# A one-core Perceiver block: more warming matmuls, head outputs in pairs, a 512-column weighted sum, and another order in the first group

## The reference, cut to what matters

```python
# layer 1
Q = layernorm(x) @ Wq + bq;  K = ctx @ Wk + bk;  V = ctx @ Wv + bv
attn = softmax(Q @ K.T) / 16
x = x + attn @ V
# layer 2, end of the delta rule: core has 8 heads of 128 x 128
core = core * rsqrt(mean(core * core, -1) + 1e-6) * gate_norm_w
core = core * silu(z)
h = resid + core.reshape(1, 128, 1024) @ W_out
```

## Time and profile before

| | |
|---|---|
| three runs | 228.18, 228.83, 229.16 us; median 228.83 us |
| profiled execution | 228.96 us, span 227.1 us |
| PE busy | 218.2 us (96% of the span), 1530 instructions |
| DVE busy | 146.8 us (65%), 349 instructions |
| ACT busy | 145.9 us (64%) |
| POOL busy | 133.4 us (59%) |
| DMA | 52.94 MB, mean 233 GB/s |

### The profile page before, as it was taken

One profiled execution on the slowest core, in us unless ns is written; L12 is line 12 of the kernel. 1 busy time (PEld: TensorE's weight loads), 2 busy tenths in 40 slices (PEclk: granted clock), 3 DMA queues, 4 the chain that ended last, 5 costly groups with the idle time before them and its releaser, 6 DMA issues.

```text
span 227.1 us, 4168 instructions
## 1 busy us (share of the span) xinstructions
PE 218.2 (96%) x1530; PEld 193.9 (85%) x1530; DVE 146.8 (65%) x349; ACT 145.9 (64%) x270; POOL 133.4 (59%) x87
## 2 busy tenths in 40 slices
PE   7999999999999999999999999959999999999994
PEld 6955888888888888989899999747899999999993
DVE  3035676666666666945996776775425579788783
ACT  3068777777778887636785676874327758677570
POOL 1045899888888888950599957390001525555550
PEclk9999999999999999999999999999999999999999
DMA  6999999999999901999700000000890677960000
GB/s 203 399 426 419 419 409 420 398 407 403 419 417 412 405 13 19 352 412 416 291 4 1 1 3 0 3 0 1 330 411 14 211 332 281 416 229 0 3 0 23
DMA packets 8532, 52.94 MB, mean 233 GB/s; under 512 B 953, under 2 KB 1217, under 8 KB 6466
## 3 DMA queue, kind: packets, MB, share of 16 engines
q1 hardware_dynamic: 8496, 52.68, 58.4%
q10 hardware_dynamic: 18, 0.01, 0.0%
HBM read 52.56 MB, written 0.13 MB: 232 GB/s over the span
## 4 chain that ended last, share of the span: by engine, by line
PE 78%; DVE 15%; ACT 3%; issue 2%; DMA 1%; POOL 0%; ACTq 0%; DVEq 0%
PE psum L507 24%; PE psum L599 13%; PE psum L873 8%; PE psum L502 7%; PE psum L575 6%; PE psum L735 3%; DVE work L1333 3%; PE psum L748 3%; PE psum L554 2%; PE psum L818 2%; DVE hh L1472 2%; DMA early_sb<-in_early 1%; PE psum L616 1%; PE psum L498 1%; DVE smalls L1222 1%
## 5 line engine op out<-in xcount | busy, mean ns | idle before, releaser
L405 POOL TENSOR_TENSOR ctx_lo<-ring,ctx_hi 128x1792 fp32r<-128x1792 f32 x13 | 52.6, 4044 | 13.8 <-ACT ctx_hi L943 13.8
L490 POOL TENSOR_TENSOR h_lo<-ring,h_hi 128x512 fp32r<-128x512 f32 x16 | 24.7, 1544 | 44.2 <-ACT h_hi L1162 38.1
L507 PE MATMUL psum<-xT,late_sb 128*128 128x128 f32 x224 | 26.4, 276 | 0.1
L507 PEld LDWEIGHTS psum<-xT,late_sb 128*128 128x128 f32 x224 | 25.6, 192 | 0.3 <-DVE xT L1529 0.3
L1222 DVE TENSOR_REDUCE smalls<-psum 128x1 f32<-128x896 f32 x14 | 15.3, 1092 | 15.3 <-PE psum L575 9.1
L507 PE MATMUL psum<-late_sb,work 128*128 128x448 f32 x60 | 24.7, 540 | 0.0
L950 ACT ACTIVATE probsT_hi<-psum 128x512 fp32r<-128x512 f32 (+1 forms) x26 | 12.7, 541 | 16.3 <-PE psum L502 16.3
L943 ACT ACTIVATE ctx_hi<-ring 128x1792 fp32r<-128x1792 f32 x13 | 22.1, 1701 | 0.0
L1246 DVE TENSOR_TENSOR probsT_lo<-psum,probsT_hi 128x512 fp32r<-128x512 f32 (+1 forms) x26 | 15.0, 619 | 6.6 <-ACT probsT_hi L950 6.6
L502 PE MATMUL psum<-early_sb,work 128*128 128x128 f32 x115 | 16.2, 274 | 0.3 <-DVE work L1457 0.2
L507 PEld LDWEIGHTS psum<-late_sb,work 128*128 128x128 f32 x60 | 10.5, 190 | 6.7 <-issue 6.7
(11 more groups left out here) (288 smaller groups left out, 522.9 us busy)
## 6 DMA issues: line engine op xcount, KB each, us to landing
late_sb<-in_ctx_T SPq DMA_DIRECT2D x14, 896.0 KB, 9.0
ring<-in_ctx SPq DMA_DIRECT2D x14, 896.0 KB, 7.8
late_sb<-in_late SPq DMA_DIRECT2D x10, 825.0 KB, 9.1
late_sb<-in_experts SPq DMA_DIRECT2D x8, 1024.0 KB, 6.0
late_slots<-in_experts SPq DMA_DIRECT2D x8, 1024.0 KB, 7.1
early_sb<-in_early SPq DMA_DIRECT2D x1, 512.0 KB, 3.8
early_sb<-in_early SPq DMA_DIRECT2D x1, 465.0 KB, 6.2
work<-in_levels SPq DMA_DIRECT2D x1, 416.0 KB, 7.3
```

What stands on the lines that cost most here:

```text
L405: nc.gpsimd.tensor_tensor(ctxNv[1][:, r % 2], ring[:, r], ctxNv[0][:, r % 2], ALU.subtract).then_inc(s["ctx_lo"], 1)
L490: nc.gpsimd.tensor_tensor(hT[1][:, e % 2, at, :], h32[:, at, :], hT[0][:, e % 2, at, :], ALU.subtract).then_inc(s["h_lo_done"], 1)
L507: last = nc.tensor.matmul(o, lhs(c), rhs(c), start=(c == 0), stop=(c == n - 1))
```

## The change: what it does

Four things are changed together.

1. `keep_warm(6)` before the rows becomes `keep_warm(7)` and `tick(2)`.
2. In the first group, ACT takes the exponential before `ctx_hi`. The group's `ctx_lo` is made by DVE and no longer by POOL, and POOL waits for it.
3. `ctx_hi` and `ctx_lo` lie side by side for each tile, so that one matmul of 512 columns takes hi*hi and hi*lo; lo*hi stays at 256 columns. The two halves of the bank are added by DVE in two steps, of which the second waits for the first. The last group is as before.
4. The head outputs go to four banks, in pairs. Gates and squares are done by pairs, the mean of squares of the first four heads stands ahead of the copy of the transposed heads, and PE projects the first heads before it transposes the second four.

```diff
-Y_BANKS = (0, 7, 1, 2, 3, 5, 4, 6)
+Y_BANKS = (1, 2, 5, 0, 6, 3, 7, 4)
+O_BANKS = (5, 0, 6, 7)
...
-            ctxN = parts(overlay, "ctx", 2 * GT * D)
+            ctxN = overlay.enter_context(nc.sbuf_tensor("ctx_parts", [P, 2 * GT * 2 * D], F32R))
...
+        def head_core(h):
+            return bank[O_BANKS[h // 2]][:, h % 2 * P:(h % 2 + 1) * P]
...
-            ctx_lo_parts(0, 0)
+            pool.wait_ge(s["ctx_lo"], 1)
...
-            keep_warm(6)
+            keep_warm(7)
+            tick(2)
...
+                def both(t):
+                    return nc.tensor.matmul(o[:, 0:2 * D], probsT[0][:, t, :], ctx_both[:, r % 2, t, :], start=(t == 0), stop=(t == GT - 1))
+
+                for q, tiles in ((1, range(4)), (2, range(4, GT))):
+                    pe.wait_ge(s["probsT_hi"], g * 2 + q)
+                    for t in tiles[:3 if q == 1 else 2]:
+                        both(t)
+                    pe.wait_ge(s["probsT_lo"], g * 2 + q)
+                    for t in tiles:
+                        nc.tensor.matmul(o[:, 0:D], probsT[1][:, t, :], ctxNv[0][:, r % 2, t, :], start=False, stop=False)
+                    last = both(tiles[-1])
                 last.then_inc(s["pv_done"], 1)
...
-                for k in range(4):
-                    last = nc.tensor.matmul(bank[5 + b][:, k * P:(k + 1) * P], Z[:, 4 * b + k, :], Bv[:, 4 * b + k, :], start=True, stop=True)
-                last.then_inc(s["o_mm"], 1)
...
+                for h in range(4 * b, 4 * b + 4):
+                    if h == 6:
+                        pe.wait_ge(s["zo_done"], 2)
+                        core_transposes(0)
+                    last = nc.tensor.matmul(head_core(h), Z[:, h, :], Bv[:, h, :], start=True, stop=True)
+                    if h % 2:
+                        last.then_inc(s["o_mm"], 1)
...
+            pe.wait_ge(s["coreT_dve"], 1)
+            for h in range(0, 2):
+                project_out(h)
+            pe.wait_ge(s["zo_done"], 4)
             core_transposes(1)
...
-            ctx_hi_parts(0, 0, 16, first=True)
             exps(0, 0, first=True)
+            ctx_hi_parts(0, 0, 16, first=True)
...
-            core_squares(0)
+            for pair in range(4):
+                core_squares(pair)
             act.wait_ge(s["core_T"], 2)
...
-            core_squares(1)
...
-                V.scalar_tensor_tensor(O[:, :], O[:, :], s_("al", b, b + 1), bank[6 + b][:, 0:D], ALU.mult, ALU.add).then_inc(s["acc_done"], 1)
+                link(V.scalar_tensor_tensor(O[:, :], O[:, :], s_("al", b, b + 1), bank[6 + b][:, 0:D], ALU.mult, ALU.add))
+                V.tensor_tensor(O[:, :], O[:, :], bank[6 + b][:, D:2 * D], ALU.add).then_inc(s["acc_done"], 1)
...
             sums(0, 0, first=True)
+            dve.wait_ge(s["ctx_hi"], 1)
+            V.tensor_tensor(ctxNv[1][:, 0], ring[:, 0], ctxNv[0][:, 0], ALU.subtract).then_inc(s["ctx_lo"], 1)
             probs_lo_parts(0)
...
-            gate_output(0)
-            gate_output(1)
+            for pair in range(3):
+                gate_output(pair)
+            mean_squares(0)
             dve.wait_ge(s["core_T"], 1)
...
-            mean_squares(0)
+            gate_output(3)
             dve.wait_ge(s["h0_done"], 1)
             for h in range(HV):
-                if h == 3:
+                if h == 2:
                     mean_squares(1)
```

More of the change, by code:

```diff
@@ L160, in perceiver @@
         probs = R2[:, 5888:5888 + GK]
-        ctxNv = [part[:, :].rearrange("p (b t d) -> p b t d", b=2, d=D) for part in ctxN]
+        ctx_both = ctxN[:, :].rearrange("p (b t e) -> p b t e", b=2, e=2 * D)
+        ctxNv = [ctx_both[:, :, :, part * D:(part + 1) * D] for part in range(2)]
         Tv = [part[:, :].rearrange("p (b c k) -> p b c k", b=2, c=DC) for part in T_parts]
@@ L592, in attend @@
                 pe.wait_ge(s["ctx_lo"], g + 1)
[L593 to L600, removed]
+                o = bank[6 + r % 2]
+                def both(t):
[8 more added lines that the diff above has]
+                    last = both(tiles[-1])
                 last.then_inc(s["pv_done"], 1)
@@ L758, in _, with core_transposes @@
                 last.then_inc(s["zt_mm"], 1)
+            def core_transposes(b):
+                transposes([(bank[3 + b][:, k * P:(k + 1) * P], core[:, 4 * b + k, :]) for k in range(4)], s["core_T"])
             for b in range(2):
@@ L951, in probs_hi_parts @@
                                          ACT.Copy).then_inc(s["probsT_hi"], 1)
+            exps(0, 0, first=True)
             ctx_hi_parts(0, 0, 16, first=True)
-            exps(0, 0, first=True)
             probs_hi_parts(0, first=True)
@@ L1103, in _, with core_squares @@
             nc.scalar.activation(Z[:, 4:8, :], bank[4][:, :].rearrange("p (h t) -> p h t", h=4), ACT.Copy, scale=-1.0).then_inc(s["zb_done"], 1)
[L1105 to L1108, removed]
+            def core_squares(pair):
+                act.wait_ge(s["zo_done"], pair + 1)
+                for h in (2 * pair, 2 * pair + 1):
+                    last = nc.scalar.activation(squares[:, h, :], head_core(h), ACT.Square, accum_out=s_("ms", h, h + 1))
                 last.then_inc(s["osq_done"], 1)
-            core_squares(0)
+            for pair in range(4):
+                core_squares(pair)
             act.wait_ge(s["core_T"], 2)
@@ L1452, in mean_squares, with gate_output @@
                                        ALU.mult, ALU.add).then_inc(s["ms_done"], 1)
[L1454 to L1457 removed]
+            def gate_output(pair):
+                dve.wait_ge(s["o_mm"], pair + 1)
+                dve.wait_ge(s["zs_done"], pair // 2 + 1)
+                at = slice(2 * pair, 2 * pair + 2)
+                V.tensor_tensor(core[:, at, :], bank[O_BANKS[pair]][:, 0:2 * P].rearrange("p (h t) -> p h t", h=2), zs[:, at, :],
                                 ALU.mult).then_inc(s["zo_done"], 1)
[L1460 to L1461 removed]
+            for pair in range(3):
+                gate_output(pair)
+            mean_squares(0)
             dve.wait_ge(s["core_T"], 1)
```

16 lines of the change are left out of this document (5 added, 11 removed).

## The result

The changed kernel took 226.63 us (median of five runs, 226.23 to 229.91) against 228.99 for the kernel before (228.18 to 229.16). The ratio is 0.9898, with a 95% interval from 0.9876 to 0.9920. That is faster by 2.4 us, where 223.5, 5.3 us less, was predicted. The direction held, and the time lies in the range, but the size was wrong by more than half.

The account below looks back on a forecast made before the run. PE was taken to bound the kernel, with 78% of the chain against DVE's 15%. From the profiled 228.96, less 3.6, 0.5 and 1.2, came 223.7, on the median's scale 223.5 us; range 222.8 to 228.1.

Parts of the forecast that it names:

- Part 3: The start: longer warming raises PE's clock early and the first group is reordered; 3.6 us gained.
- Part 1: The weighted sum with 512-column matmuls: 0.9 us gained over groups 0 to 10, 0.4 lost in group 11, so -0.5.
- a rise at 6.2: The start: if the clock's level rises only then, scores start at about 9.2 and the gain is 3.3 us.
- The early case that I took: The start: clock up while rows are transposed, scores from 8.44, gain 4.0 at best, 3.6 taken; chance 0.48.
- the new order: First group: late clock, no loss; early clock, exponential no longer held from 13.4 to 14.5, DVE's `ctx_lo` 2.3 us.
- The second addition: Steady groups on DVE: 0.44 us plus 0.03 wait, 0.47 more in a pause of 0.58, so hidden in groups 0 to 10.
- the rival in which it does not fit: Second addition on DVE takes 0.72 and overruns its pause: +2.6 us, 230.7 in all; chance 0.06.
- The saving per group: PE's weighted sum: seven pairs become seven 512-column matmuls, 0.08 us saved per group.
- PE's work behind the wait: End of layer 1: after `probsT_lo` of group 12 PE needs 1.74 us instead of 1.82, so 0.4 lost in all.
- Part 2: The head outputs in pairs, first mean ahead of the copy, earlier product with `W_out`: 1.2 us gained.
- The late rise: Rival at the start: the clock rises late all the same, 0.3 us lost there, 227.4 in all; chance 0.36.
- the heads gain little: Rival: late clock, and ACT or POOL's power holds the later sums, 0.9 of 1.2 goes, 228.3; chance 0.10.

Follow-up runs that it names:

- e1: The kernel before with only the longer warming at the start: 227.81 us against 228.51, ratio 0.9998.
- e4: The changed kernel with ACT's `ctx_hi` of the first group put ahead of the exponential again, DVE still making `ctx_lo`: 225.92 us, ratio 0.9929 to the kernel before.
- e6: The changed kernel with the whole old first group (`ctx_hi` first, `ctx_lo` on POOL): 226.11 us, ratio 0.9929 to the kernel before.
- e7: The kernel before with the new head outputs and the longer warming, old weighted sum and first group: 225.64 us, ratio 0.9881.
- e8: The changed kernel with layer 1's end reordered: `probsT_lo` ahead of the addition, last probabilities ahead of ACT's factor: 225.32 us, ratio 0.9879 to the kernel before.
- e11: The kernel before with the longer warming, the new head outputs and the reordered end of layer 1, old weighted sum and first group: 225.24 us, ratio 0.9871.
- e2: The kernel before with only the new head outputs in pairs, old short warming: 226.46 us, ratio 0.9938.
- e3: The kernel before with only the new 512-column weighted sum: 230.11 us, ratio 1.0104.
- e9: The kernel before with a write of zeros that nothing reads behind each DVE addition to `O`, 13 in all: 228.88 us, ratio 0.9990.
- e5: The changed kernel itself, run again on another set's chip: 226.67 us, ratio 0.9951 to the kernel before.

## Why the prediction was wrong in size

Of the 3.0 us that are missing, 1.8 are Part 3's and 1.1 Part 1's.

**Part 3 is the step that failed most: 3.6 predicted, 1.79 measured.** Two things were wrong in it. The first is the moment. I took a rise during the transposes and scores from 8.44; here it came after them, and the scores at 9.67, later than the 9.2 that I gave for a rise at 6.2. The 0.3 to 0.6 that the longer warming delays the transposes has to be paid in this case as well (0.49 here), and I had counted it only for the late rise. e1, with the same start and the old order, gains 2.61. The early case that I took does occur: in e4, e6, e7, e8 and e11 the two transposes start 0.27 or 0.28 apart and not 0.48. Even there the scores start at 8.82 to 9.20 and not at 8.44. The Trainium skill, in *TensorE: Matmul & The Clock Gate*, Part 1, says that the moment differs between runs of one kernel; the profiles agree, with scores from 8.82 to 12.00 behind the same warming.

The second is the new order, which I thought harmless or helpful. I had the first maximum ready at 13.4, where ACT's `ctx_hi` would still hold the exponential. For scores at 8.44 that was nearly right: in e2, with scores at 8.58, the maximum is ready at 13.67 and the exponential waits for `ctx_hi` until 14.01. With scores at 9.67 the maximum is ready only at 14.8, and `ctx_hi` fits ahead of it. What I had at nothing is the other side: with `ctx_hi` behind the exponential, POOL's next `ctx_lo` and `ctxT_lo` come 1.0 late, and `ctxT_lo` meets DVE's part of it. That cost 0.82 here, and 0.4 or more in every profile where DVE makes this `ctx_lo`. DVE's `ctx_lo` itself took 2.02, priced 2.3. Without the new order e2 reaches W1 at 25.09, 3.40 sooner than the kernel before, close to the 3.6: the rise was priced rightly for a lucky execution.

**Part 1, -0.5 predicted, +0.60 measured.** The second addition was right (0.42 against 0.44) and hidden in the steady groups as argued; the rival in which it does not fit is refuted. The saving per group was 0.06 on PE's weighted sum, not 0.08. The Trainium skill, in *TensorE: Matmul & The Clock Gate*, Part 1, has 2.5 ns a matmul; measured are 0.06 / 7, some 9 ns, nearer to the 12 taken from rows. Of the groups' 0.9 only 0.35 arrived: in the traces every second group keeps its 6.10 from one weighted sum to the next, for a reason that stays open. At the end of layer 1 the second addition cost 0.45 of the 0.47 predicted. What I had wrong there is PE's work behind the wait. I had it shrink, from 1.82 to 1.74, but the 1.82 of the earlier trace rows run to the end of the last matmul. From start to start it is 1.66 before and 1.87 now (92.79 to 94.66), since a matmul of 512 columns has been put behind the first half's `lo` matmuls, so that two products more follow the wait. So the end lost 0.59 and not 0.4, and e8, in which PE does not wait there, wins back 0.83. And 0.36 came from the place in DVE's list, of which nothing in the trace of before warned.

**Part 2 was right: -1.2 predicted, -1.08 measured.** POOL's first power begins 2.68 after the first head output, predicted 2.61. PE's product came as forecast, 3.32 against 3.26, but could be read 0.3 later. Its larger effect was not in the sum: with the new heads and PE's pause down to 0.97 the falls of the clock there nearly all went; a fall costs 1.26 in e1, and more in e3 and e9.

**The rivals.** The late rise, at 36%, is what some executions of the changed kernel are: 229.91 in the first five, 228.56 to 229.93 in three of eleven in e5. They take longer than its 227.4, since parts of the change cost more than it assumed. It is not what sets the median, but its 227.4 for the time was nearer than mine, for another reason. That the heads gain little is refuted. I also took the kernel before as always late, from one profile. At least a third of its executions are early (29 of 85 under 227.6), and lose a part of that again at the heads.

## What to carry to other kernels

Price a gain of the clock from several executions of the kernel before: a mean granted clock of 0.992 or 0.985 beside a time tells of a fall that a profile at 1.00 does not show. Two edits can depend on each other through the clock: warming at the start paid only together with the head outputs, far behind it, that shortened a pause of PE. When an operation is moved behind another one, work out when that one's last input is ready in each case of the clock, look whether the operation sat in a gap of its own, and follow what comes late behind it.

## What the runs showed that I had not expected

- PE's clock can fall after a pause of 2.5 us (in e1, e3 and e9, not in the profile before) and stayed at 2.4 GHz after one of 0.97 to 1.23 in every profile with it. Why the fall comes with nearly every early start and only some late ones (e3's profile is one) stays open.
- DVE pauses at places in its list, ahead of the 192nd and the 320th recorded instruction, so a longer list puts the pause in front of other work. It costs nothing in e9, and 0.15 to 0.36 in rows of operations that others wait for.
- A subtraction of 384 columns on DVE took 1.30 us instead of 0.55 beside POOL's of 512 columns, which took 1.30, about its mean of 1.28.
